# A decoder layer on one core: operands of the first batch built on chip, products of weights moved into the attention, and the low parts, squares and state part of a cross unit shared out anew

## The reference, cut to what matters

```python
x = layernorm(x + attn(x))         # causal, 16 heads of 16, softmax over keys
x = layernorm(x + xattn(x, ctx))
x = layernorm(x + ffn(x))          # 16 experts of 64, the best 4 of a token

def xattn(slots, P):               # both batches x 256 x 256
    Pn = rmsnorm(P, input_norm_w);  k = Pn @ Wk.T;  v = Pn @ Wv.T
    for _ in range(3):
        q = rmsnorm(slots, slot_norm_w) @ Wq.T
        a = softmax((q @ k.T) * SCALE, axis=-2)       # over slots
        a = a / (a.sum(-1, keepdims=True) + 1e-6)
        gx = (a @ v) @ wih.T + bih;  gh = slots @ whh.T + bhh
        r = sigmoid(xr + hr);  z = sigmoid(xz + hz)
        n = tanh(xn + r * hn)
        slots = (1 - z) * n + z * slots
    return slots
```

## Time and profile before

| | us |
|---|---|
| median of 3 runs | 743.46 |
| lowest and highest | 742.22, 750.99 |
| profiled execution, its own time | 744.92 |
| its span, first to last instruction | 743.2 |

### The profile page before, as it was taken

How to read it: one execution, slowest core, us unless ns; L and a number is a source line. 1 busy time by engine, 2 the same in 40 slices (tenths; PEclk the granted TensorE clock), 3 DMA queues, 4 the chain that set the end, 5 groups by cost and what they waited for, 6 DMA issues and landing times. The chain is left out here.

```text
span 743.2 us, 14255 instructions
## 1 busy us (share of the span) xinstructions
PE 660.8 (89%) x5256; PEld 606.2 (82%) x5256; DVE 473.7 (64%) x1005; ACT 319.2 (43%) x704; POOL 231.9 (31%) x257
## 2 busy tenths in 40 slices
PE   5568899898989999998999989999888895999996
PEld 4446677676768999998999989999888885989896
DVE  3445375666735767777677876768767676556553
ACT  3215354454654444552445524545344433162441
POOL 8113233333352431312213022231343304250533
PEclk9779799999999999999999999999999998899999
DMA  7674456367200400000000000000000000000000
GB/s 242 209 201 141 141 159 186 82 190 203 59 16 2 142 1 1 15 16 0 0 0 14 14 0 0 0 0 0 1 1 1 2 1 0 15 16 30 0 28 29
DMA packets 25679, 40.11 MB, mean 54 GB/s; under 512 B 2336, under 2 KB 11424, under 8 KB 25632
## 3 DMA queue, kind: packets, MB, share of 16 engines
q1 hardware_dynamic: 25632, 39.49, 17.8%
HBM read 24.67 MB, written 14.68 MB: 53 GB/s over the span
## 5 line engine op out<-in xcount | busy, mean ns | idle before, releaser
L1153 DVE TENSOR_REDUCE neg_max<-bank 128x2 f32<-128x512 f32 (+1 forms) x96 | 65.4, 690 | 78.9 <-PE bank L1641 50.9
L403 PE MATMUL bank<-slots_hl,whhT_hl 128*128 128x256 f32 x864 | 115.0, 292 | 0.0
L403 PEld LDWEIGHTS bank<-slots_hl,whhT_hl 128*128 128x128 f32 x864 | 109.4, 196 | 1.4 <-DVE vg_hl L1222 0.2
L1922 PE MATMUL bank<-attn_hl,vg_hl 128*128 128x256 f32 x864 | 109.2, 286 | 0.7 <-ACT attn_hl L729 0.6
L1922 PEld LDWEIGHTS bank<-attn_hl,vg_hl 128*128 128x128 f32 x864 | 104.6, 194 | 1.4 <-ACT attn_hl L729 0.8
L765 ACT ACTIVATE pT<-bank 128x512 f32<-128x512 f32 x96 | 56.9, 597 | 64.1 <-PE bank L1654 48.5
L604 POOL TENSOR_SCALAR_AFFINE_SELECT pT<-pT 128x512 f32<-128x512 f32 x64 | 40.5, 636 | 117.2 <-ACT pT L765 117.2
L692 POOL TENSOR_TENSOR slots_hl<-slots,slots_hl 128x512 fp32r<-128x512 f32 x16 | 20.4, 1277 | 134.0 <-ACT slots_hl L729 134.0
L715 POOL TENSOR_TENSOR hid_hl<-hid,hid_hl 128x512 fp32r<-128x512 f32 x32 | 40.8, 1287 | 44.2 <-ACT hid_hl L729 44.1
L403 PE MATMUL bank<-x2T_hl,keys_hl 128*128 128x256 f32 x384 | 51.8, 290 | 1.1 <-ACT hid L1055 1.1
L403 PEld LDWEIGHTS bank<-x2T_hl,keys_hl 128*128 128x128 f32 x384 | 48.6, 195 | 1.9 <-ACT hid L1055 1.7
(11 more groups left out here) (187 smaller groups left out, 1334.8 us busy)
## 6 DMA issues: line engine op xcount, KB each, us to landing
q_rows<-q_hl SPq DMA_DIRECT2D x24, 256.0 KB
k_rows<-k_hl SPq DMA_DIRECT2D x24, 256.0 KB
q_op<-q_rows SPq DMA_DIRECT2D x32, 192.0 KB, 3.3
k_op<-k_rows SPq DMA_DIRECT2D x16, 384.0 KB, 5.3
xT_in<-in_xT_dram SPq DMA_DIRECT2D x4, 512.0 KB, 5.5
x_in<-in_x_dram SPq DMA_DIRECT2D x8, 256.0 KB, 7.0
c_in<-in_ctx_dram SPq DMA_DIRECT2D x8, 256.0 KB, 4.6
out_dram<-y_out SPq DMA_DIRECT2D x8, 256.0 KB, 2.1
```

The lines of the kernel that those rows point to most:

```text
L403: mm = pe.matmul(dst, left(a), right(b), start=first and n == 0, stop=last and n == 2, skip_group_check=True)
L1153: dve.tensor_reduce(dst, src, AX.X, ALU.max, negate=True).then_inc(max_ok, 1)
L1922: mm = pe.matmul(halves(b)[:, m, :], vg_hl[:, j, v_part, 3 * t + r, q:q + P], attn_hl[:, j, at_part, t, :], start=n == 2 and a + m + t == ...
```

## The change

- **Start.** The first pair's text is loaded and projected by batch (`project_first`). For batch 0 `q_op` and `k_op` are built on chip: PE multiplies 32 rows of `q_hl` or `k_hl` by `spot`, a matrix of zeros and ones made by POOL, which puts each part in its rows (`set_rows`, 12 fills of two matmuls of 512 columns); ACT copies 8 of the results (`set_queries`), DVE 4 (`set_keys`). Batch 0 isn't written to DRAM or read back; batch 1 is, as before. The products of weights become entries "w" 0 to 4 beside quads -1 to 2, with their splits by ACT and DVE.
- **Squares.** POOL adds the two halves of the squares (`add_squares`), and PE takes the mean by 2 matmuls for 4.
- **Candidate.** ACT makes 0.5 (hn + bhh) out of PSUM (`hidden_out`, one more wait and two more instructions a unit on ACT), and DVE forms the product with r by one operation, (t + 1) times that, in place of three.
- **Order on DVE.** `soft_sum` comes after the candidate's first addition, `mean_square` ahead of `weights`, and `attn_lo` of units 1 to 4 moves from POOL to DVE behind `weights`, where it waits for ACT's high part. At the turn both norms' moments come first, and the next pair's first `soft` stands between `norm(0)` and `norm(1)`. On PE, `text(0)` comes ahead of the mean squares and state products of the next pair's units.
- **Experts' weights.** Their low parts move from POOL (four subtractions of 128x1024) to DVE (eight of 128x512), behind `soft_sum` and behind `attn_lo` of the last pair.

The diff, cut to its core:

```diff
+            def first_text_hi(batch):
+                act.wait_ge(xT_first[batch], 16)
+                copy(xT_hl[:, HI, :, batch * T:(batch + 1) * T], xT_in[:, :, batch * T:(batch + 1) * T]).then_inc(xT_hi, 1)
...
+            def set_rows(s):
...
+                for use in range(3):
+                    fill = 3 * s + use
+                    b = set_bank(s, use)
...
+                    rows = slice(32 * s, 32 * s + 32)
+                    hl, high, low = (q_hl, use, 2 + use) if use < 2 else (k_hl, 4, 5)
+                    pe.matmul(bank[b][0:K_ROWS, :], spot[rows, high, :], hl[rows, HI, 0, :, :], start=True, stop=False)
+                    pe.matmul(bank[b][0:K_ROWS, :], spot[rows, low, :], hl[rows, LO, 0, :, :], start=False, stop=True
+                              ).then_inc(set_mm, 1)
...
+            def set_queries(s):
+                for e in range(2):
+                    act.wait_ge(set_mm, 3 * s + e + 1)
+                    copy(q_op[0:K_ROWS, 0, e, 2 * s:2 * s + 2, :], halves(set_bank(s, e))[0:K_ROWS, :, :]).then_inc(set_q, 1)
...
+            def set_keys(s):
+                dve.wait_ge(set_mm, 3 * s + 3)
+                dve.tensor_copy(k_op[0:K_ROWS, 0, 2 * s:2 * s + 2, :], halves(set_bank(s, 2))[0:K_ROWS, :, :]).then_inc(set_k, 1)
...
             pe.wait_ge(prep_dve, 2)
+            pe.wait_ge(xT_lo, 1)
+            project_first(4, 0, 0)
+            pe.wait_ge(prep_dve, 3)
+            project_first(6, 0, 1)
             pe.wait_ge(xT_lo, 2)
...
+            project_first(5, 1, 0)
+            set_rows(0)
+            project_first(7, 1, 1)
+            for s in range(1, 4):
+                set_rows(s)
...
+        FIRST_BESIDE = {(-4, 0): [("v", 0), ("v", 1)], (-1, 2): [("w", 0)], (0, 2): [("w", 1)], (1, 0): [("w", 2)],
+                        (1, 2): [("w", 3)], (2, 2): [("w", 4)]}
...
-            write_q(0, 0)
-            write_k(0, 0)
-            sp.wait_ge(consts, 15)
-            operands(0, 0)
-            operands(0, 1)
+            load_xT(1)
             write_q(0, 1)
             write_k(0, 1)
-            load_xT(1)
             load_x(0)
             load_x(1)
...
+                    if (quad, third) == (-4, 0):
+                        dve.wait_ge(prep_act, 4)
+                        step(sub_hi(whhT_hl[:, LO, :, :], st_hhT[:, :, :], whhT_hl[:, HI, :, :]))
...
+            def add_squares(i, u):
+                pool.wait_ge(sq_ok, due(UNITS, i, u + 1))
+                pool.tensor_tensor(sq[:, 0, :], sq[:, 0, :], sq[:, 1, :], ALU.add).then_inc(sq_sum, 1)
...
-                    for c in range(NC):
-                        mm = pe.matmul(bank[b][:, t:t + 1], sq[:, c, t * P:(t + 1) * P], mean_col[:, :], start=c == 0, stop=c == 1)
+                    mm = pe.matmul(bank[b][:, t:t + 1], sq[:, 0, t * P:(t + 1) * P], mean_col[:, :], start=True, stop=True)
...
+            def hidden_out(i, u):
+                act.wait_ge(hn_mm, due(UNITS, i, u + 1))
+                act.wait_ge(g_ok, due(UNITS, i, u))
+                for c in range(NC):
+                    r = act.activation(hidden[:, c, :], halves(6)[:, c, :], ACT.Identity, scale=0.5, bias=bhh_col[:, 2 * NC + c:2 * NC + c + 1])
+                r.then_inc(hb_ok, 1)
...
+                    if u < 4:
+                        hidden_out(i, u + 1)
...
                     if u + 1 < UNITS:
                         attn_hi(i, u + 1)
...
                     dve.wait_ge(r_ok, due(UNITS, i, u + 1))
-                    dve.tensor_scalar(gate_r[:, :, :], gate_r[:, :, :], 0.5, 0.5, ALU.mult, ALU.add).then_inc(cross_chain, 1)
...
+                    dve.wait_ge(hb_ok, due(UNITS, i, u + 1))
+                    dve.scalar_tensor_tensor(gate_r[:, :, :], gate_r[:, :, :], 1.0, hidden[:, :, :], ALU.add, ALU.mult).then_inc(g_ok, 1)
...
+            def attn_lo(i, u):
+                j = u % 2
+                dve.wait_ge(at_hi, due(UNITS, i, u + 1))
+                sub_hi(attn_hl[:, j, LO, :, :], attn[:, j, :, :], attn_hl[:, j, HI, :, :]).then_inc(at_lo, 1)
...
                     reset_gate(u)
-                    if u + 1 < UNITS or not last:
-                        soft_sum(i, u + 1)
                     gates(u)
...
                         totals(i, u + 1)
-                        weights(i, u + 1)
                     if u + 2 < UNITS:
                         mean_square(i, u + 2, 0)
+                    if u + 1 < UNITS:
+                        weights(i, u + 1)
+                    if u + 1 < UNITS - 1:
+                        attn_lo(i, u + 1)
+                    if u < 4 and last:
+                        expert_weights_lo(2 * u)
...
+                    text_moments(0)
+                    text_moments(1)
                     norm(0)
+                    soft(i, UNITS + 1)
                     norm(1)
```

More of the change, by code:

```diff
@@ L527, in _ @@
                     if 1 <= 2 * period + 3 < B:
-                        after(sp, consts, 17 if period == -1 else 0)
+                        after(sp, consts, 14 if period == -1 else 0)
                         operands(2 * period + 3, 0)
@@ L688, in cross @@
                         context_scale(i)
+                    if u < UNITS - 2:
+                        add_squares(i, u + 2)
+                    elif u == 4 and not last:
+                        add_squares(i, UNITS)
                     if u < UNITS - 2:
@@ L930, in _ @@
                         text_out(2 * period - 2)
-                    elif key == (4, 2) and 1 <= period + 2 < PAIRS:
+                    elif key == (4, 2) and 2 <= period + 2 < PAIRS:
                         text_hi(2 * (period + 2))
+                    elif (quad, third) == (-3, 0):
+                        for piece in range(2, 4):
+                            text_hi(piece)
                     elif key == (5, 0) and 0 <= 2 * period < B:
                         heads_out(2 * period, 1)
-                    elif key == (5, 1) and 1 <= period + 2 < PAIRS:
+                    elif key == (5, 1) and 2 <= period + 2 < PAIRS:
                         text_hi(2 * (period + 2) + 1)
@@ L949, in _ @@
                         exps(quad, third)
+                    for name, n in beside(quad, third):
+                        if name == "w":
+                            context_weights_hi(n)
                 first_context(quad)
@@ new lines, in context_weights_lo @@
+            def context_weights_lo(n):
+                dve.wait_ge(prep_act, n + 7)
+                b = BESIDE_BANK["w", n, 0]
+                if n == 0:
+                    for c in range(NC):
+                        step(dve.scalar_tensor_tensor(qk_w_hl[:, LO, c, :], halves(b)[:, c, :], input_col[:, c:c + 1],
+                                                      f32(qk_w_hl[:, HI, c, :]), ALU.mult, ALU.subtract))
+                else:
+                    c, blocks = VALUE_BLOCKS[n - 1]
+                    step(dve.scalar_tensor_tensor(v_w_hl[:, LO, c, blocks], bank[b][:, 0:blocks.stop - blocks.start],
@@ L1344, in _ @@
                         maxima(quad + LEAD, third)
+                    if (quad, third) == (-4, 0):
+                        dve.wait_ge(prep_act, 4)
+                        step(sub_hi(whhT_hl[:, LO, :, :], st_hhT[:, :, :], whhT_hl[:, HI, :, :]))
+                        dve.wait_ge(prep_act, 6)
+                        step(sub_hi(eselT_hl[:, LO, :, :], st_esel[:, :, :], eselT_hl[:, HI, :, :]))
+                    for name, n in FIRST_BESIDE.get((quad, third), ()):
+                        if name == "v":
+                            values_out(n, BESIDE_BANK["v", n, 0])
+                        else:
+                            context_weights_lo(n)
                     if key == (0, 0) and 0 <= 2 * period - 2 < B:
@@ L1474, in gates @@
                     dve.tensor_tensor(gate_r[:, :, :], halves(7), gate_r[:, :, :], ALU.add).then_inc(np_ok, 1)
+                    if u + 1 < UNITS or not last:
+                        soft_sum(i, u + 1)
                     if last and u == UNITS - 1:
@@ new lines, in context_weights @@
+            def context_weights(n, b):
+                if n == 0:
+                    pe.wait_ge(w_in[5], 32)
+                    for c in range(NC):
+                        for o in range(NC):
+                            mm = pe.matmul(halves(b)[:, c, :], st_wk[:, o, c * P:(c + 1) * P], st_wq[:, o, :], start=o == 0, stop=o == 1)
+                else:
+                    pe.wait_ge(w_in[6], 32)
+                    c, blocks = VALUE_BLOCKS[n - 1]
+                    for o in range(NC):
+                        mm = pe.matmul(bank[b][:, 0:blocks.stop - blocks.start], st_wv[:, o, c * P:(c + 1) * P], st_ihT[:, o, blocks],
+                                       start=o == 0, stop=o == 1)
+                mm.then_inc(prep_mm, 1)
```

292 lines of the change are left out of this document (175 added, 117 removed).

## The result

The changed kernel takes 692.32 us (median of 4 runs, 690.52 to 697.22) against 742.84 of the kernel before on the same chip: a ratio of 0.931 [0.923, 0.940], faster. In six further runs it was 694.79 and the ratio 0.934 [0.931, 0.938]. Its profiled execution took 690.52 us, span 688.8; before it was 744.92 and 743.2, so 54.4 us of span are to be explained. PE's mean granted clock rose from 0.954 to 0.984.

A forecast was written before the change was run, and what follows sets the result against it. PE was taken to bound the cross part except at some places, something else the start; 16.5 + 1.3 + 2.4 + 11 + 10.9 + 1.5 = 43.6 us off 744.92 gave 701.3, as median 700, range 684 to 718.

The forecast's parts named there:

- The start: Up to the first turned fill: batch 0's DRAM trip removed, fill at 37 for 55.46, 16.5 us won net (5 to 22).
- the rival in which the start stays with DMA: Start: batch 1's operands land about as late as before, first turned fill at 50, 5 us won; 712, chance 0.14.
- The regular unit: Cross part: shorter chain from mean squares to inputs, 0.1 us a unit, 1.3 us over twelve units (0 to 8).
- the collision of the weights with POOL's root: Regular units: POOL's reciprocal root, released by the same mean square, holds DVE's second weights instruction; 0.57 us (0 to 0.69).
- The rival "no collision": Regular units and last pair: POOL's root on two columns holds nothing, 9 us more won; 691, chance 0.2.
- The mean squares: Two more mean squares a pair with no weights behind them: 6 x 0.4 = 2.4 us won.
- The reset product: Regular unit, DVE: it takes 0.69 for 0.43 and 0.87; the 0.65 gained pays for `soft_sum`'s new place.
- the slower rival: Units: `attn_lo` on DVE waits for ACT and delays `soft` and what follows, 60 us lost against 44; 760, chance 0.03.
- The turns: Turns between pairs: wait falls from 3.0 to 1.3 us, 3.7 us won a turn, 11 in all (6 to 13).
- the rival in which the second norm keeps the wait long: Turns: the wait ends on the second norm, not `soft`; 8 of the 11 us stay; 708, chance 0.08.
- The last pair: POOL's 128x1024 subtractions go; units of 12.6 us for 15.3, 10.9 us won over four (7 to 13).
- the rival of a loss in small waits: Cross units: new small waits cost PE its clock, 1.6 us in half of 20 units, 16 us; 716, chance 0.09.

The follow-up runs named there:

- start_only: The kernel before with the new start alone, nothing of the rest: 728.93 us, ratio 0.983.
- w_early: The changed kernel with the products of weights beside quads -4 and -3 rather than -1 to 2: 694.80 us, ratio 0.937.
- ffn_pool: The changed kernel with the low parts of the experts' weights back on POOL, in four subtractions of 128x1024: 704.03 us, ratio 0.950.
- wide_add: The changed kernel with one more POOL addition of 128x256 per unit, ahead of the root and released by the same mean square: 706.56 us, single run.
- whh_pool: The changed kernel with the low part of `whhT` made by POOL instead of DVE: 692.97 us, against 694.79 for the unaltered kernel beside it.
- squares_pe: The changed kernel with the mean of squares by four matmuls on PE and no addition on POOL: 699.73 us, ratio 0.942.
- reset_three: The changed kernel with the reset product by three DVE instructions out of PSUM and no `hidden_out` on ACT: 710.49 us, ratio 0.958.
- attn_lo_pool: The changed kernel with the low part of the attention weights (`attn_lo`) on POOL in every unit: 701.07 us, ratio 0.943.
- turn_old: The changed kernel with the old order at the turn, each norm in one piece and the next `soft` behind both: 700.30 us, ratio 0.942.

## Why the prediction was right, and where its terms were off

700 was predicted and 692.3 to 694.8 measured, inside the range. By the profiled executions 43.6 us were forecast and 54.4 came; the table above shows that nearly all of the difference is in the regular units and the last pair, 22.8 for 12.2.

**The start** was right: first natural fill at 20.69 (forecast 21), first turned at 39.11 (37), first totals 16.5 earlier (16.5). That the last agrees to a tenth is luck: with the same code the first totals came at 227.7 and 233.5, and start_only won 14. The two stages were as the prediction had them, though: up to the first turned fill DMA is no longer waited for, and DVE's low parts with POOL's collision (1.75, 1.16, 2.72) are in its way. Batch 1's operands were read from 27.5 on, so the rival in which the start stays with DMA fell. The products of weights cost 2 by the prediction; w_early shows that they are not free earlier either, but no run shows what they cost where they are.

**The regular unit** held the step that failed: the collision of the weights with POOL's root, taken at 0.57 a unit, is 0. The prediction gave 0.67 a unit for its absence, and 0.76 was measured (12.45 to 11.69, the mean of the 11). The rival "no collision" was the right one, with its mechanism, and its 691 is close to the 692.3 to 694.8; its price covered the collision alone. From the mean squares to the inputs 2.23 us pass, where the prediction had 3.0 with the collision and 2.44 without (weights 0.87 for the 0.95 assumed, PE's reading 0.1 shorter). I had put two rows side by side, 3.18 us of weights beside a 2.56 us POOL instruction, and carried their rule over to an instruction on two columns. The bounds were right, 0 and 0.69; the choice between them had no row near it. The Trainium skill, "SBUF — State Buffer", section "SBUF: two separate sides", says that whichever of the two starts first holds the pair for the whole instruction. By ffn_pool, wide_add and whh_pool the trace agrees for wide ones, in both directions. For the short root it does not as regards DVE: it runs beside the weights in 16 units, the weights take 0.87 as they do alone (0.88), and 0.16 to 0.19 us are lost on POOL's side. One reading is that the root needs the port for a small part of its 0.69 us only; no run here separates that.

**The mean squares** by two matmuls were taken at 0.40 in two places of a pair, the fifth unit's interval and the turn, and in regular units as covered by the chain over the weights. squares_pe shows 0.5 in the first of them, nothing at the turn, and 0.44 in a regular unit too: with the new order on DVE that chain starts behind the mean squares as PE's own work does, so nothing covers them. **The reset product** was said to pay with 0.65 for the new place of `soft_sum`; reset_three costs some 0.6 a regular unit (12.25 for 11.6), so that step was right. **`attn_lo` on DVE** was the slower rival's mechanism. DVE's wait for ACT is there (0.70), but it ended long before `soft` had to run, and attn_lo_pool shows the move as a gain of 0.4 a unit, to which the prediction gave nothing.

**The turns** were right in kind and close in size: a wait of 0.69 (forecast 1.3), full clock behind it, 12.6 us with the intervals behind them (forecast 11 and some of the squares' 2.4). turn_old gives 9.0 for the order of moments, norms and `soft`. That order was enough, and the rival in which the second norm keeps the wait long fell.

**The last pair** won 14.4 for 10.9: units of 11.7 for the 12.6 forecast, by the missing collision and because the delay of `soft` costs nothing. It is there: `soft` starts at 500.04, 0.5 us behind the copy of the scales, since DVE is still at the subtraction begun at 499.43. But the reciprocal of the sum is done at 503.03, ahead of the totals at 503.17 for which PE is free only then.

```profile
502.87 0.16 DVE L1357 RECIPROCAL s_inv<-s_sum 128x2 f32<-128x2 f32 x1
...
503.17 1.10 PE L1943 MATMUL bank<-attn,s_inv 128*128 128x256 f32 x4
```

**The clock** did not suffer anywhere in the 20 units; the rival of a loss in small waits had no waits to work on.

The undone edits sum to 52 us (7.9, 9.0, 9.1, 6.3, 6.5 and 13.6) where the cross part won 37. That is no contradiction: in the changed kernel PE is without a pause, so each edit taken back becomes the bound by itself. That several taken back at once would share one wait is argued; no run takes back two. None of the six can be left out without a loss.

**Left open:** the first totals of one kernel vary by almost 6 us, by a clock of 0.66 around 35 us and by one late read of keys near 169 us; what brings on the one or the other, no run shows.

## What to carry to other kernels

When several small chains end within a few tenths of each other ahead of the bounding engine, cost each against the others' ends and not against the wait that the profile names: undone singly, six edits of this change cost 6 to 14 us each. Before pricing a collision of VectorE and GpSimd, look for a row with operands of about that width: a GpSimd instruction of 128x256 or more held VectorE's two-input instructions here until it was about done, one of 128x2 didn't. Moving work off VectorE to GpSimd was no relief in whh_pool, where VectorE had a two-input instruction of its own to do at that moment.

## What the runs showed of the hardware

- A POOL power on 128x2 beside DVE's weights took 0.87 for 0.69 to 0.71 and left them at 0.87 (0.88 with POOL idle); a POOL addition of 128x256 at the same place made them 1.37, a subtraction of 128x1024 made them 2.93, and one of 128x1536 held a DVE subtraction of 128x32 for 2.67 us. The lock works the other way too: behind DVE's 1.75 us subtraction POOL's took 2.72, for 1.28 alone (the same form in whh_pool at 26.01 us).
- Three waits of 2.99 to 3.00 us before the change were each followed by state products of 6.1 us, at a granted clock of 0.72. The same three waits in start_only, 3.00 us each, were followed twice by 6.12 and once by 4.59 us at 1.00. In turn_old three waits of 2.66 to 2.70 us behind the same work were followed once by a clock of 0.69 and twice by 1.00, and four waits of 1.78 to 1.86 us in ffn_pool by 1.00 each time. Before the change a wait of 2.38 us was followed by a clock of 0.71, one of 2.21 by 1.00. So the length of the wait alone did not decide it; what else does, no run here shows.
